# Two-layer graph attention with mixture-of-experts: rows and weights loaded earlier at the stage borders, lists and routing written otherwise

## The reference

```python
# layer 0
gat = segment_sum(alpha * (h @ Wfc)[src], dst)            # 8 heads of 64
x = elu(gat) + h
y = relu(x @ w1.T + b1) @ w2.T + b2 + x                   # 512 -> 256 -> 512
x = layernorm(y) * ln_g + ln_b  (+ the layer's input)
# 16 experts, each takes the 468 tokens with the highest gate (softmax(x @ gate_weight))
x[token] += gate * (gelu(x[token] @ w1[e] + b1[e]) @ w2[e] + b2[e])
# layer 1
x = layernorm(segment_sum(alpha * (x @ W)[src], dst) + ...) * ln_gamma + ln_beta (+ input)
# 8 experts, each token takes the two best of softmax(x @ Wr.T + br), weights normalised
out = sum_e combine[:, e] * (gelu(x @ W1[e] + b1[e]) @ W2[e] + b2[e])
```

## Time and profile before

| what | value |
|---|---|
| median of 3 runs | 3113.9 us (3112.03 to 3117.18) |
| profiled execution, its own time | 3120.04 us |
| its span, first to last instruction | 3118.3 us |
| busy: PE, DVE, POOL, ACT | 2675.0 (86%), 1871.9 (60%), 1623.8 (52%), 727.3 us (23%) |
| HBM traffic | 163 GB/s over the span |
| mean granted TensorE clock | 0.938 |

### The profile page before, as it was taken

One profiled execution on the slowest core, in us unless ns is written; L12 is line 12 of the kernel. 1 busy time (PEld: TensorE's weight loads), 2 busy tenths in 40 slices (PEclk: granted clock), 3 DMA queues, 4 the chain that ended last, 5 costly groups with the idle time before them and its releaser, 6 DMA issues. The chain is left out here.

```text
span 3118.3 us, 40184 instructions
## 1 busy us (share of the span) xinstructions
PE 2675.0 (86%) x10312; PEld 1261.7 (40%) x10313; DVE 1871.9 (60%) x3301; ACT 727.3 (23%) x1355; POOL 1623.8 (52%) x1517
## 2 busy tenths in 40 slices
PE   6899799899987981999999698898988989656998
PEld 4444332222223541555554344433223223244776
DVE  6785876666666867533231456697666666675343
ACT  2002310111111771121111110032111111253665
POOL 4674277777772000344443047507777777613665
PEclk8999899999998985899999799999999999867999
DMA  7483277777774431365565449437777777575776
GB/s 268 113 137 107 79 211 211 211 211 210 211 210 146 143 118 61 92 153 146 139 152 125 158 145 174 99 140 204 211 210 211 211 211 210 153 251 135 134 135 111
DMA packets 341635, 511.11 MB, mean 164 GB/s; under 512 B 174570, under 2 KB 179930, under 8 KB 340966
## 3 DMA queue, kind: packets, MB, share of 16 engines
q0 software_dynamic: 115872, 317.04, 40.2%
q1 hardware_dynamic: 95462, 183.58, 17.2%
q10 hardware_dynamic: 130144, 8.52, 2.8%
HBM read 422.33 MB, written 86.65 MB: 163 GB/s over the span
## 5 line engine op out<-in xcount | busy, mean ns | idle before, releaser
L1226 POOL DMA_INDIRECT zg<-z_rows,src_groups x940 | 898.0, 955 | 480.4 <-issue 273.2
L1305 PE MATMUL bank<-zg,aggregate_onehot 128*128 x1888 | 941.6, 625 | 105.5 <-DVE zg L1273 98.0
L1273 DVE TENSOR_TENSOR zg<-zg,bank 128x1024 f32<-128x1024 f32 x470 | 573.4, 1220 | 409.8 <-DMA zg<-z_rows,src_groups 409.6
L1305 PEld LDWEIGHTS bank<-zg,aggregate_onehot 128*128 128x128 f32 x1888 | 305.4, 189 | 740.0 <-issue 726.8
L828 PE MATMUL bank<-alpha,front_table 128*64 128x512 bf16 x2304 | 268.5, 388 | 20.1 <-DVE alpha L681 20.1
L355 PE MATMUL bank<-zg,x 128*128 128x512 f32 x480 | 219.3, 613 | 11.8 <-PEq L371 11.2
L2185 PE MATMUL bank<-exp_w,exp_h_t 128*117 128x512 f32 x512 | 225.8, 595 | 0.7 <-ACT exp_h_t L2132 0.7
L2039 POOL DMA_INDIRECT x_rows<-exp_y,exp_add_tok x64 | 137.0, 2141 | 159.1 <-DVE exp_y L2092 146.3
L2177 PE MATMUL bank<-exp_xg_t,exp_w 128*128 128x468 f32 x512 | 205.8, 561 | 0.7 <-ACT exp_xg_t L2121 0.7
L828 PEld LDWEIGHTS bank<-alpha,front_table 128*64 128x64 bf16 x2304 | 133.4, 112 | 152.4 <-issue 51.6
L1251 DVE TENSOR_TENSOR aggregate_onehot<-bank,columns 128x256 f32<-128x256 f32 x472 | 192.0, 416 | 0.0
(11 more groups left out here) (453 smaller groups left out, 3342.2 us busy)
## 6 DMA issues: line engine op xcount, KB each, us to landing
exp_w<-in_L_ffn_w SPq DMA_DIRECT2D x32, 1024.0 KB, 7.6
zg<-src_key SPq DMA_DIRECT2D x48, 512.0 KB, 4.9
zg<-z_rows,src_groups POOLq DMA_INDIRECT x940, 3.7
zg<-src_tile SPq DMA_DIRECT2D x96, 128.0 KB, 3.4
exp_w<-in_L_ffn_W SPq DMA_DIRECT2D x2, 4096.0 KB, 15.8
x_rows<-zg SPq DMA_DIRECT2D x10, 768.0 KB, 3.5
hn_rows<-zg SPq DMA_DIRECT2D x10, 768.0 KB, 4.0
x<-x_rows SPq DMA_DIRECT2D x5, 1536.0 KB, 14.5
```

The source lines that it names most:

```text
L1226: pool.indirect_dma_start(zg[:, r, j, :], None, k.z_rows[:, :], bass.IndirectOffsetOnAxis(k.src_groups[:, n:n + 1], 0)).then_inc(gathered[ ...
L1273: v.tensor_tensor(z, z, bcast_last(scales[:, at:at + J * H], DH), ALU.mult).then_inc(msg_ready, 1)
L1305: mm = nc.tensor.matmul(k.banks[:, bass.ds(bank, 1), :].rearrange("p a n -> p (a n)"), onehot_at(n)[:, j, :], zg[:, bass.ds(at, 1), j, :]. ...
```

## The change

- The first two x blocks of `finish_layer0` are loaded by SP at the end of `aggregate`, as soon as the slots that they lie on are free (`EarlyLoads0`). The stage itself begins with `w1`, `b1`, `w2`, which now lie in `alpha`; the three rows, two x blocks and last `gw` follow, `gw` on a semaphore of its own. The first block is joined and handed on by tile.
- In layer 1 the gain and offset rows are loaded into a freed slot of `zg` and the router's bias into a tile of its own (`EarlyLoads1`), and POOL adds the offset to blocks 0 and 1 behind its last gather.
- The first x block of layer 1's front is loaded in two halves with a semaphore each.
- Lists: only expert 0's `by_quarter` stands before the first list, those of experts 1 and 2 behind it. `sum_list` takes 32 columns of `by_quarter` as the weights and moves the 117 columns of `placed`, into one of four column groups in turn; ACT copies the four parts, and one f32 matmul with `fold` adds them. The order of the first three lists on DVE is changed. The gathers of expert 0 have a semaphore per quarter. PE's rounds are unrolled.
- `route1`: both slots in one multiply and one reduction; the tokens beyond the last node are prepared while ACT exponentiates; the third pass over `named` goes to ACT in 30 pieces; `te` is made on one partition by one compare and one reduction instead of seven compares.

```diff
+class EarlyLoads0:
+    groups = ((NGR - SLOTS, NGR - SLOTS + 1), (NGR - SLOTS + 2, NGR - SLOTS + 3))
...
+    def load(self, sp, n):
+        sp.dma_start(self.x[n], self.I["x"][n * BT:(n + 1) * BT, :]...).then_inc(self.x_in[n], 16)
...
+class EarlyLoads1:
+    groups = ((NGR - SLOTS, NGR - SLOTS), (NGR - SLOTS + 1, NGR - SLOTS + 1))
...
+    def add_offset(self, n):
+        a = self.k.x[:, n * TB:(n + 1) * TB, :]
+        self.k.nc.gpsimd.tensor_tensor(a, a, self.offset.unsqueeze(1).to_broadcast([P, TB, D]), ALU.add).then_inc(self.offset_added, 1)
+    def add_offsets(self, pool):
+        pool.wait_ge(self.rows_loaded, 16 * 2)
+        for n in range(EARLY_OFFSETS):
+            self.add_offset(n)
...
@@ aggregate, gpsimd and sync
+                if layer == 1:
+                    pool.wait_ge(zeroed, EARLY_OFFSETS * TB)
+                    early.add_offsets(pool)
...
+                for u in range(2):
+                    first, last = early.groups[u]
+                    sp.wait_ge(summed, sp.value_load(k.group_freed[0:1, last:last + 1], min_val=1, max_val=STEPS))
+                    early.load(sp, u)
...
@@ finish_layer0
-                load_x(0)
-                load_x(1)
...
+                early.load_weights(sp)
...
-                act.wait_ge(w_loaded, 16 * 4)
+                act.wait_ge(w_loaded, 16 * 3)
...
@@ choose_tokens
-                values_by_quarter(k, chain, slice(0, LISTED_FIRST))
+                values_by_quarter(k, chain, slice(0, 1))
...
@@ experts0, vector
                 place_list(0, 0)
+                v.tensor_reduce(fold[:, :], k.ident...[:, 0:QF, :], AX, ALU.add).then_inc(fold_ready, 1)
+                chain(values_by_quarter(k, chain, slice(1, LISTED_FIRST)))
                 v.tensor_copy(k.ps[7][:, 0:PQ], k.iota[:, 0:PQ]).then_inc(lanes_ready, 1)
-                place_list(1, 1)
                 read_list(0, 0)
                 v.tensor_copy(gather_tok[:, 0, :], tokens[:, 0:Q0]).then_inc(gather_tok_ready, 1)
+                place_list(1, 1)
...
@@ experts0, tensor
-                        mm = nc.tensor.matmul(k.ps[bank][0:PQ, 0:Q0 * 5], placed[:, b, t, :],
-                                              k.by_quarter[:, bass.ds(n, 1), t, :, :]...,
-                                              start=(t == 0), stop=(t == NT - 1))
+                        g, width = t % KC, GROUP if t < NT - 1 else QF
+                        mm = nc.tensor.matmul(k.ps[bank][g * GROUP:g * GROUP + width, 0:PQ], values_of(n, t, width), placed[:, b, t, :],
+                                              start=(t < KC), stop=(t >= NT - KC), skip_group_check=True)
...
+                def fold_list(n, bank):
+                    pe.wait_ge(parts_copied, n + 1)
+                    nc.tensor.matmul(k.ps[bank][0:PQ, 0:QF], parts[:, :], fold[:, :], start=True, stop=True).then_inc(list_folded, 1)
...
+                            if q == 2 and u < lists:
+                                pe.wait_ge(xg_t_ready, i * (U * Q0) + (u * Q0 + Q0 + 2))
+                                fold_list(i * U + (u + AHEAD0), 1)
...
-                with pe.Fori(0, LISTING) as i:
+                for i in range(LISTING):
                     body(i, U, False)
...
@@ route1
-                dve.wait_ge(br_loaded, 16)
...
-                for s in range(2):
-                    chain(v.tensor_tensor(tmp[:, :, :], oh[:, s, :, :], slot_e[:, :, :], ALU.mult))
-                    chain(v.tensor_reduce(slot_f[:, :, s], tmp[:, :, :], AX, ALU.add))
...
+                chain(v.tensor_tensor(tmp[:, :, :, :], oh[:, :, :, :], slot_e..., ALU.mult))
+                chain(v.tensor_reduce(slot_f..., tmp[:, :, :, :], AX, ALU.add))
+                chain(v.tensor_tensor(slot_f[:, :, :], slot_f[:, :, :], beyond[:, :, :], ALU.add))
...
-                chain(v.tensor_tensor(by_tile, by_tile, tile, ALU.mult))
...
+                for t in range(NT):
+                    by_tile = named[:, 2 * t:2 * t + 2, 1, :]
+                    nc.scalar.activation(by_tile, by_tile, ACT.Copy, scale=float(t + 1)).then_inc(tile_named, 1)
...
+                        pe.wait_ge(tile_named, (n + WB + 1) // 2)
```

More of the change, by code:

```diff
@@ L377, in load_x @@
                     full = SBT - 1 if layer == 0 and b == last else SBT
+                    if layer == 1 and b == 0:
+                        for j in range(0, SBT, X_FIRST):
+                            sp.dma_start(k.x[:, j:j + X_FIRST, :], rows[j * P:(j + X_FIRST) * P, :].rearrange("(t p) d -> p t d", p=P)).then_inc(x_first if j == 0 else x_loaded[b], 16)
+                        return
                     sp.dma_start(k.x[:, b * SBT:b * SBT + full, :],
@@ L1133, in front, with aggregate @@
         return Softmax
-def aggregate(k, name, layer, softmax):
+def aggregate(k, name, layer, softmax, early):
     nc = k.nc
@@ L1328, in finish_layer0 @@
+def finish_layer0(k, I, early):
     nc = k.nc
@@ L1616, in _, with finish_layer1 @@
                 logits(NB - 1)
-def finish_layer1(k, I):
+def finish_layer1(k, I, early):
     nc = k.nc
@@ L1665, in _ @@
                 sp.wait_ge(x_stored, 16 * NB)
+                sp.wait_ge(bias_loaded, 16)
             @block.gpsimd
             def _(pool):
-                pool.wait_ge(rows_loaded, 16 * 2)
-                for n in range(NB):
-                    nc.gpsimd.tensor_tensor(block_of(n), block_of(n), rowp[:, 1, :].unsqueeze(1).to_broadcast([P, TB, D]), ALU.add).then_inc(offset_added, 1)
+                for n in range(EARLY_OFFSETS, NB):
+                    early.add_offset(n)
             @block.vector
@@ L1725, in _ @@
                 act.wait_ge(rows_loaded, 16 * 2)
-                nc.scalar.copy(gain, rowp[:, 0, :]).then_inc(gain_copied, 1)
+                nc.scalar.copy(gain, early.gain).then_inc(gain_copied, 1)
                 for n in range(NB):
@@ L1989, in experts0 @@
         listed = sb("listed", [PQ, AHEAD0 + U, Q0, 5], F32)
+        QF, GROUP = Q0 * 5, 32
+        parts = sb("parts", [P, PQ], F32)
+        fold = sb("fold", [P, QF], F32)
+        values_of = lambda n, t, width: k.by_quarter[:, :, :, :, :].rearrange("p e t q f -> p (e t q f)")[:, n * (NT * QF) + t * QF:n * (NT * QF) + t * QF + width]
         part = sb("part", [PQ, 2, Q0], F32)
@@ L2020, in _, with gather @@
             def _(pool):
-                def gather(n, u):
+                def gather(n, u, first=False):
                     wait_here(pool, gather_tok_ready, n + 1, passed)
@@ L2369, in _ @@
                                     ALU.is_equal).then_inc(low_ready, 1)
-                chain(v.memset(te[:, :], 0.0))
-                for e in range(E1 - 1):
-                    chain(v.scalar_tensor_tensor(te[:, :], tile_at[:, :], ends[:, e:e + 1], te[:, :], ALU.is_ge, ALU.add))
+                chain(v.tensor_tensor(passed_ends[:, :, :], bcast_last(tile_at[0:1, :], E1 - 1), ends[0:1, 0:E1 - 1].unsqueeze(1).to_broadcast([1, MT, E1 - 1]), ALU.is_ge))
+                chain(v.tensor_reduce(te[:, :], passed_ends[:, :, :], AX, ALU.add))
                 chain(v.tensor_copy(k.tile_expert[:, :], te[0:1, :]))
```

209 lines of the change are left out of this document (130 added, 79 removed).

## The result

The change made the kernel faster: 3084.36 us median (3078.65 to 3088.65, four runs) against 3115.54 us (3112.03 to 3121.56, four runs), a ratio of 0.9897 with a 95% interval from 0.9874 to 0.992. That is 31.2 us; the forecast was 27.3 us and 3086.6. The profiled execution of the changed kernel took 3078.65 us (span 3077.0, mean granted clock 0.942), the one before 3120.04 us (span 3118.3). Between these two lie 41.4 us, ten more than between the medians, so the two traces can't be subtracted without asking which stages differ by chance.

The account below looks back on a forecast made before the run. No single engine was taken as the bound, but the last-ending wait in each stage. Terms -6.3, 0, -2.2, -5.5, -4.8, -8.5 sum to -27.3 us off the median 3113.9: 3086.6 us, range 3081 to 3093, with rivals 3079 to 3099.

Parts of the forecast that it names:

- First finishing stage, -6.3: Weights loaded first, x blocks early: ACT's first take 6.7 us sooner, less 0.4 for delayed last gathers.
- the bound of 2.1: End of the first aggregation: upper bound in us for the early x blocks' delay, one block at 375 GB/s.
- Second front, 0: Front of layer 1, first x block in two halves: no change, between -1 and +0.6 us.
- First lists, -2.2: Before expert 0: transposes released by the third list instead of the gathers, 2.2 us sooner, between 0 and -4.5.
- Lists in the loop, -5.5: Expert loop on PE: each of thirteen lists costs 1.26 us instead of 1.68, gaining 0.42 each.
- my lower bound of -8: Thirteen lists in the expert loop: largest gain, in us, with 30 matmuls in 0.8 us at some 27 ns each.
- the unrolled rounds save nothing: PE's rounds in the expert loop: no gain from unrolling, since PE had no gap at the branch.
- Second finishing stage, -4.8: Early gain and POOL offsets let DVE start at 2705.3 instead of 2709.19 and skip a 0.88 us wait for POOL.
- DVE is the bound for the rest of the stage: Second finishing stage: DVE sets the pace after its start, so all of the 4.8 us is kept.
- `route1`, -8.5: `route1`'s DVE chain: bias wait 2.27 us gone, moved pass 4.4, merged operations 0.9, `te` 1.05, small operations 0.1.
- PE warming sooner: Rival: shorter gaps ahead of two hidden layers return 2.2 and about 2.5 us, lists 2 more: 3080, chance 0.08.
- The lists' rival: Rival: list matmuls stay at 56 ns, fold and form change come on top, +4.7 instead of -5.5: 3098, chance 0.12.

Follow-up runs that it names:

- the run with old lists: Changed kernel with the old list sum (one-hot as weights, 20 moved columns, no column groups, no fold), straight PE rounds kept: 3097.72 us, ratio 0.9938.
- the run with x in the stage: Changed kernel with x blocks 0 and 1 issued in the first finishing stage right behind `w2`, none early: 3087.08 us, ratio 0.9904.

## Why the prediction was right, step by step

The total was right within 2.2 us of the first median, but partly by luck. The forecast difference of 27.3 us stood on a median of 3113.9; against the medians beside which the changed kernel was measured it was short by 3.9 us, in the second group by 6.1. And two errors cancelled: the lists gave 5.2 us more than their term, the second border 4.8 less.

- **First finishing stage, -6.3.** Measured: -7.5 in the stage, +1.9 in the aggregation (611.5 to 611.9 us in three traces, then 613.1 to 614.0 in seven of eight), together -5.6. The arithmetic of bytes held: ACT's first take 5.5 us after the first issue against 5.9 forecast. The mis-sized part is the early x blocks, taken at 0.4 because traffic was half free; free bandwidth wasn't the question, since the waits of 2.6 us and more came whatever the bytes. The 1.9 us lie inside the bound of 2.1, and about half of them is in doubt, since the aggregation without an early load took 612.57.
- **Second front, 0.** Nothing shows against it: over all traces this front took 352.7 to 357.6 us before and 350.2 to 355.5 with the change, so the trace's -6.7 is within chance.
- **First lists, -2.2.** Measured -3.1. The change of hands came as forecast, from DMA to the third list. But the parts were weighed wrongly: the form of the sum was put at 0.8 of the gain and the run with old lists gives it 2.5, so the smaller `by_quarter` and the new order bring the other 0.6.
- **Lists in the loop, -5.5.** The right mechanism, the wrong size, and outside my lower bound of -8: -9.9 for the form. The pace is 0.60 us for 30 matmuls, 20 ns each, where I took 1.0 us and bounded it by the 27 ns of the earlier trace rows. That row, 1.76 us over 60, is 29 ns, and it has 128-column weights; it was no lower bound for 32-column weights in four groups. And "the unrolled rounds save nothing" missed 0.8 us: the periods between the first and the thirteenth are 0.04 to 0.2 us longer in the loop, and I had looked only at the last ones.
- **Second finishing stage, -4.8.** This term failed: the two stretches together took 684.0, 685.5 and 687.1 us without the early work and 684.1 to 689.1, with a median of 684.9, with it. The step was "done at 2702, before the aggregation ends at 2704". POOL's adds took their 6.8 us as reckoned, but POOL reached the border 6.7 us later than they end, which costs 2.2 us; the aggregation with the loads of gain, offset and bias, for which I had no term, is longer by about as much even without adds (601.66 us without early offsets against 599.38 to 599.93 before); and the 0.88 us that DVE no longer waits for POOL came back in `fin_shift`, 2.39 us instead of 1.60. "DVE is the bound for the rest of the stage" had this wrong: for its first blocks the bound is POOL's adds, two per block. What did come is the early start: the first `fin_shift` ends 9.93 us into the stage instead of 14.2 to 14.3.
- **`route1`, -8.5.** Measured -9.0; the terms as listed add up to 8.7, not 8.5. ACT's pieces go out every 0.21 us, nearer to the extrapolated 0.25 than to the 0.37 of the earlier trace rows, and are covered.

Of the rivals, PE warming sooner came closest to the trace (3080 against 3078.65), but its cause is half borne out: the first hidden layer began at half clock in four of ten traces with the new form and at full clock in six, which would be 1.1 us on the mean, an estimate from 1.8 us in six of ten. The hidden layer of the finishing stage, which the prediction put at the same half clock, ran before at a mean granted clock of 0.68 and then at 0.77, 7.89 against 6.97 us. The lists' rival fell by its own test. The 62 ns per small matmul that the prediction weighed are not there, and the trace also undercuts the other rule. The Trainium skill (TensorE: Matmul & The Clock Gate, section "Wait — 56ns, not 53.3ns?") puts the floor at 25 ns however small the matmul. Here thirty pass in 0.60 us, 20 ns each, in four column groups, and the measurement decides.

By the terms as measured: -5.6, -3.1, -9.9 and -0.8 in the loop, 0 at the second border, -9.0, which is -28.4; the medians say 31.2 and, in the second group, 33.4. The few microseconds left over are of the size by which the fronts and the first hidden layer differ between executions.

## What to carry to other kernels

Work that is moved behind an engine's last instruction is only free if the engine's way out of the stage is free too: look at when an idle engine reaches the border, not at when its last instruction ends. Where two engines hold each other up, taking work from one ahead of the stage moves the wait and doesn't remove it: look at which instructions end together. A load beside a stream of gathers was followed here by the wait for one gather, whatever its bytes, so halving it gained nothing; whether it would be free far from the end no run tests. And a difference between two traces is to be held against the same stage in traces of unchanged code first: here a stage without any edit took 355.4 to 361.1 us.

## What the runs showed of the hardware

- POOL, after 3.4 us adds behind a row of indirect gathers, reached the stage's border 6.7 us after the last add in six traces with two adds and in the one with three (6.71 and 6.72 in those shown).
- A DVE operation of three columns with both operands in SBUF (`fin_shift<-mv,rstd`) took 0.35 to 3.75 us beside POOL's f32 adds, mostly 1.59 or 2.39 in the first block, and 0.16 after them. In all fourteen traces each one beside the adds ended 0.02 us after a POOL add. The large f32 multiplies of DVE with one operand in a PSUM bank (`zg<-zg,bank`) kept their 1.22 us beside POOL's adds.
- A wait of 2.6 to 4.6 us for one gather follows a load on SP's queue in each of the 21 aggregations that have one near their end, and ends 5 to 7 us behind its issue, for one block of x, for two, and for two parameter rows alone. Such waits also occur without a load ahead of them: 2.69 and 2.73 us, 30 and 44 us before the end of two aggregations of the kernel before with written-out rounds, and 3.11 us, 17.6 us before the end, in the run with x in the stage. So the load isn't shown to be their only cause.
- 32-column weights in four column groups: 20 ns per bf16 matmul of 117 moved columns in the loop and 33 ns (0.98 us for 30) at the half clock of the first lists, against 56 ns (1.68 us per list) and 106 ns (3.17 us for 30) in the old form.
- The granted clock rises from half to full at different moments of the same code: 0.9 us before the first hidden layer (12.80 us) in one trace, 3.6 us after its start (14.60 us) in the one with one early offset.
